# Seven blocks of queries in each pass of the unit loop, in place of one

## The chip, the cores and the metric

The kernel runs on one core of a Trainium2 chip. The metric is the time of one execution in device microseconds (us), the median of several runs. Engines are named as the profile names them: PE (matmul), PEld (its weight loads), DVE (vector), ACT (scalar, activations), POOL (GpSimd), SP (the queue that issues DMAs). A "q" behind an engine's name (ACTq, SPq) marks an instruction of its sequencer: a register operation, a branch, a semaphore operation or the issue of a DMA.

## The reference

x has 2 batches of 4096 tokens with 256 features. The first half is an attention with 16 heads of 16 features, whose weights are not a softmax but a sigmoid:

```
x_norm = layernorm(x, gamma, beta)
q, k = l2_normalize(x_norm @ w_q), l2_normalize(x_norm @ w_k);  v = x @ w_v      (per head)
resonance = 0.5 + 0.5 * tanh((q k^T - 0.27) * 15)
modulation = resonance * gate_q * gate_k        (gates: 0.25 + 0.75 sigmoid(q . g_q), the same for k)
x = layernorm(x + (modulation @ v) @ w_o + b_o)
```

The second half is a feed-forward network on each token, y = down(silu(gate(x)) * up(x)) with 704 hidden features, whose inputs and weights are rounded to 4-bit blocks of 16, and another layernorm of x + y.

## The kernel before, in words

Every engine has its own program; semaphores tie them together. There are three stages. The first projects 16 blocks of 512 tokens and stores q, k, v and the gates in DRAM. The second, the attention, takes nearly all of the time. The third finishes the last four tiles of tokens.

The attention is cut into 64 **units**: 16 blocks of 512 queries (index j, 8 per batch), and in each of them 4 groups of heads (index g). In a unit PE computes the scores of 4 heads against 32 tiles of 128 keys (`scores`, line 1257), ACT turns them into sigmoids (line 696), and PE sums them with v (`sums`, line 1267). This goes in 44 steps: a step's ACT instruction waits for the scores (`b_sc`), and PE's scores two steps later wait for that ACT instruction (`b_act`). At the end of a unit DVE takes the sums out of PSUM (`end_unit`, line 972, the instruction that writes `fs`); there are 64 of these, so their starts mark off the units. SP then stores `fs` (line 497), loads the gates (line 521), and loads the next unit's keys, queries and values (`load_unit`, lines 472 to 478).

Beside the attention, each unit from the fifth on carries one tile of 128 tokens of the feed-forward network for an earlier block. SP loads the tile's attention result into `m_f` (`load_sums`, line 503, after the stores of line 497 and the loads of line 521 in SP's program); PE needs it after step 7 of the unit (`begin_piece`, line 1279). PE's program is in a fixed order: while it waits for `m_f`, the scores of the next steps stand behind it.

The order over units is written by `units` (line 369), which every engine calls with its own `unit(j, g)`. The first two blocks (j = 0 and 1) are written out, with Python numbers for j. The other 14 go through a hardware loop of each engine (`fori`), whose register is j; its body holds one block, that is four units. Values that depend on j (the counts that semaphores are waited for, the addresses of DMAs) are computed in registers by the engine's sequencer. DVE also counts its own chain of dependent instructions: `before` (line 1020) sets the base of the count at the head of a pass, 4 units times 45 links further in each pass.

Of the kernel before, what the change touches and what calls it, by code (L numbers as in the profile page):

```python
# [23 lines left out]
HG = 4  # L24
NG = H // HG
NS = TB * 2 * H
NUNIT = B * NG * QB
# [58 lines left out]
LAST = {9: 0, 11: 1, 13: "gates", 15: 2, 17: 3}  # L86
NTAIL = HG
LOOP_FROM = 2

PT_BANKS = (7, 0, 1, 2)
# [5 lines left out]
L_CHAIN = 45  # L97
# [28 lines left out]
def build(nc, x, w_q, w_k, w_v, g_q, g_k, w_o, b_o, gamma, beta, w_gate, w_up, w_down, out):  # L126
# [12 lines left out]
    with ExitStack() as ctx:  # L139
# [229 lines left out]
        def units(fori, unit, before=lambda r: None):  # L369

            for j in range(LOOP_FROM):
                for g in range(HG):
                    unit(j, g)
            with fori(LOOP_FROM, NUNIT // HG) as j:
                before(j - LOOP_FROM)
                for g in range(HG):
                    unit(j, g)

        def begins(j, g):  # L380

            return not isinstance(j, int) or j >= 1

        def ends(j, g):

            return not isinstance(j, int) or HG * j + g > HG
# [367 lines left out]
        def _(dve):  # L754
            chain = Chain(dve, dve_step)
# [11 lines left out]
            def quantize(dst, src, w):  # L767

                nb = w // 16
                s3, xn3, t3 = (a.rearrange("p (n e) -> p n e", e=16) for a in (src, q_xn[:, 0:w], q_t[:, 0:w]))  # L770
                scale, inv = q_s[:, 0, 0, 0:nb], q_s[:, 0, 1, 0:nb]
                xn, e, t = q_xn[:, 0:w], q_e[:, 0:w], q_t[:, 0:w]
                after(dve.tensor_reduce(scale, s3, AX_X, ALU.max, apply_absolute_value=True))
                after(dve.tensor_scalar(scale, scale, 1 / 6, QUANT_EPS, ALU.mult, ALU.max))
                after(dve.reciprocal(inv, scale))
                after(dve.tensor_scalar(inv, inv, TIE_DOWN, None, ALU.mult))
                after(dve.tensor_tensor(xn3, s3, bcast(inv, 16), ALU.mult))

                after(dve.tensor_scalar(e.bitcast(I32), xn.bitcast(I32), EXPONENT, None, ALU.bitwise_and))
                after(dve.tensor_scalar(e, e, ROUNDER, ROUNDER, ALU.mult, ALU.max))  # L780
                after(dve.tensor_tensor(t, xn, e, ALU.add))
                after(dve.tensor_tensor(t, t, e, ALU.subtract))
                return dve.tensor_tensor(dst.rearrange("p (n e) -> p n e", e=16), t3, bcast(scale, 16), ALU.mult)
# [87 lines left out]
            at = chain.n  # L871
# [10 lines left out]
            def keep_last():  # L882

                for i, what in enumerate(LAST.values()):
                    dve.wait_ge(a_last, i + 1)
                    if what == "gates":
                        wait(dve, a_outg, 16 * (NBLK - 1))
                        ins = dve.tensor_copy(gT[:, :], ps[0:H, C_BANK, :])
                    else:
                        ins = dve.tensor_copy(last_pt[what], bank16(C_BANK))  # L890
                    ins.then_inc(a_lastev, 1)
# [27 lines left out]
            def end_transposes(k):  # L919
                for half in range(2):  # L920
                    dve.wait_ge(l_H, 2 * k + half + 1)
                    if half == 0:
                        dve.tensor_copy(m_hqT[:, 0:4, :].rearrange("p j n -> p (j n)"), ps[:, C_BANK, :])\
                           .then_inc(l_hT, 1)
                    else:
                        dve.tensor_copy(m_hqT[:, 4, :], ps[:, C_BANK, 0:P])  # L926
                        dve.tensor_copy(m_hqT[0:FR, 5, :], ps[0:FR, C_BANK, P:2 * P]).then_inc(l_hT, 1)  # L927

            def end_tile(k, par):
                dve.wait_ge(l_D, k + 1)  # L930

                wait(dve, l_st[par], 16 * (k // 2))
                after_fin(dve.tensor_tensor(m_xo[:, par], ps[:, C_BANK, 0:D], m_x1[:, par], ALU.add), k)  # L933
                normalize(m_xo[:, par], m_xo[:, par]).then_inc(l_out, 1)
# [5 lines left out]
            def begin_tile(k, par):  # L940
                x1 = m_x1[:, par]
                dve.wait_ge(l_P, k + 1)
                dve.wait_ge(l_xb, k + 1)
                dve.tensor_tensor(x1, ps[:, C_BANK, 0:D], m_x[:, :], ALU.add).then_inc(l_r, 1)  # L944
                dve.wait_ge(l_r, k + 1)
                after(normalize(x1, x1))
                wait(dve, l_X, k)
                to_grid(m_xq[:, :], x1, D, m_xs, m_xn[:, :], m_e[:, :], m_t[:, :]).then_inc(l_xq, 1)

            def gates(k):  # L950
                dve.wait_ge(l_X, k + 1)
                dve.tensor_copy(m_xqT[:, :, :].rearrange("p c n -> p (c n)"), ps[:, C_BANK, 0:D]).then_inc(l_xT, 1)
                for p in range(4):
                    cols = slice(p % 2 * FH, (p % 2 + 1) * FH)
                    if p < 2:
                        dve.wait_ge(l_sg, 2 * k + p + 1)
                        dve.tensor_tensor(m_tg[:, cols], ps[:, C_BANK, 0:FH], m_sg[:, cols], ALU.mult)\  # L957
                           .then_inc(l_ge, 1)
                    else:
                        dve.wait_ge(l_G, 4 * k + p + 1)  # L960
                        dve.wait_ge(l_ge, 4 * k + p)
                        dve.tensor_tensor(m_hb[:, cols], ps[:, C_BANK, 0:FH], m_tg[:, cols], ALU.mult)\  # L962
                           .then_inc(l_ge, 1)
                dve.wait_ge(l_ge, 4 * k + 4)
                wait(dve, l_H, 2 * k)
                to_grid(m_hq[:, :], m_hb[:, :], F, q_s[:, 0], q_xn[:, :], q_e[:, :], q_t[:, :]).then_inc(l_hq, 1)
# [7 lines left out]
            def keep_weights(i):  # L974

                dve.wait_ge(c_wt, i + 1)
                if i < 2:
                    ins = dve.tensor_copy(wdnT[:, 2 * i:2 * i + 2, :].rearrange("p j n -> p (j n)"), ps[:, C_BANK, :])
                elif i == 2:
                    dve.tensor_copy(wdnT[:, 4, :], ps[:, C_BANK, 0:D])  # L980
                    ins = dve.tensor_copy(wdnT[0:FR, 5, :], ps[0:FR, C_BANK, D:2 * D])
                else:
                    c, part3 = divmod(i - 3, 3)
                    if part3 < 2:
                        ins = dve.tensor_copy(wguT[:, c, part3 * F:part3 * F + 512], ps[:, C_BANK, :])
                    else:
                        for m in range(2):
                            dve.tensor_copy(wguT[:, c, m * F + 512:m * F + 640], ps[:, C_BANK, m * P:(m + 1) * P])
                        for m in range(2):
                            ins = dve.tensor_copy(wguT[:, c, m * F + 640:(m + 1) * F],  # L990
                                                  ps[:, C_BANK, 2 * P + m * FR:2 * P + (m + 1) * FR])
                ins.then_inc(c_wev, 1)

            def unit(j, g):
                u = HG * j + g
                if ends(j, g):
                    end_transposes(u - HG - 1)
                if begins(j, g):
                    begin_tile(u - HG, g % 2)
                if ends(j, g):  # L1000
                    end_tile(u - HG - 1, (g - 1) % 2)
                if begins(j, g):
                    gates(u - HG)
                if isinstance(j, int) and j == 0:
                    if g == 0:
                        keep_last()
                        dve.wait_ge(s_ffn, 16 * FFN_LOADS)
                    if g < 2:
                        for n in (range(0, W_FIRST), range(W_FIRST, DC + NW))[g]:
                            rows, w = (wdn[:, n, :], F) if n < DC else (wgu[:, n - DC, :], D)  # L1010
                            quantize(rows, rows, w).then_inc(w_q_done, 1)
                            dve.wait_ge(w_q_done, n + 1)
                    if g == 2:
                        for i in range(9):
                            keep_weights(i)
                end_unit(u)

            at = [0]

            def before(r):  # L1020
                at[0] = chain.n
                chain.start(at[0] + r * HG * L_CHAIN)

            units(dve.Fori, unit, before)
            assert chain.n == HG * L_CHAIN, chain.n
            chain.start(0)
            chain.n = at[0] + (NUNIT // HG - LOOP_FROM) * HG * L_CHAIN
            k = NT - NTAIL - 1
# [433 lines left out]
```

## Time and profile before

| | us |
|---|---|
| median of 3 runs | 4456.29 |
| lowest, highest run | 4455.4, 4465.12 |
| the profiled execution's own time | 4458.66 |
| its span, first to last instruction | 4456.9 |

| engine | busy us | share of the span |
|---|---|---|
| PE | 4149.7 | 93% |
| ACT | 4023.4 | 90% |
| DVE | 1561.7 | 35% |
| POOL | 159.3 | 4% |

The profile is of one execution. Register operations, branches, semaphore operations and the issue of DMAs are not counted as busy. The first stage ends some 320 us into the span, the attention some 4374 us into it. In the list of idle times, `A <- B` says that A was idle until B was done; "issue" stands for idle time in which the engine waited for nothing that the profile shows. PEclk is the granted share of TensorE's full clock.

### The profile page before, as it was taken

To read this page: it belongs to the slowest core of one execution; us is meant where nothing else is said; L and a number is where in the kernel's file an instruction comes from. 1 tells how busy PE (TensorE), PEld (TensorE's weight loads), DVE (VectorE), ACT (ScalarE), POOL (GpSimd) and SP (SyncE) were. 2 spreads that over 40 slices of the span, in tenths; PEclk is the share of its full clock that TensorE was granted. 3 is DMA by queue.
4 is the path that set the end of the run, shared out by engine and by line. 5 is a ranking of instruction groups with operands and counts; after the bars stand their busy time and mean duration, and the time that the engine had idled before them with its cause. 6 is when DMAs were issued, how large, how long until landed. Compare 5 with 4: busy or idle time off the path is not lost.

```text
span 4456.9 us, 80908 instructions
## 1 busy us (share of the span) xinstructions
PE 4149.7 (93%) x28776; PEld 1293.5 (29%) x28776; DVE 1561.7 (35%) x4540; ACT 4023.4 (90%) x3271; POOL 159.3 (4%) x120
## 2 busy tenths in 40 slices
PE   7978899999999999999999999999999999999997
PEld 5641222222222222222222222222222222222223
DVE  6754023332333233233332333233323323333236
ACT  4669999999999999999999999999999999999993
POOL 2330000000000000000000000000000000000001
PEclk9999999999999999999999999999999999999998
DMA  3454444334433443344334433443344334433440
GB/s 111 126 124 75 69 75 69 61 62 77 77 57 59 77 77 57 59 77 77 56 61 75 77 56 60 76 77 58 58 76 77 56 61 77 77 54 62 76 81 13
DMA packets 180058, 315.51 MB, mean 71 GB/s; under 512 B 65264, under 2 KB 141808, under 8 KB 154608
## 3 DMA queue, kind: packets, MB, share of 16 engines
q1 hardware_dynamic: 179568, 309.41, 41.2%
q8 instruction: 255, 4.18, 0.4%
q14 instruction: 235, 1.93, 0.2%
HBM read 266.82 MB, written 42.47 MB: 69 GB/s over the span
## 4 chain that ended last, share of the span: by engine, by line
PE 68%; ACT 17%; issue 9%; DVE 4%; SPq 1%; DMA 1%; POOL 0%; ACTq 0%; POOLq 0%; DVEq 0%
PE ps L1267 35%; PE ps L1257 19%; ACT room L696 16%; PE ps L1294 7%; PE ps L1317 4%; DVE room L848 1%; DMA m_f<-fused_t 1%; PE ps L1212 0%; DVE st L802 0%; DVE xnT L838 0%; PE ps L1223 0%; PE ps L1307 0%; SPq L521 0%; PE ps L1204 0%; DVE sm L763 0%
## 5 line engine op out<-in xcount | busy, mean ns | idle before, releaser
L696 ACT ACTIVATE room<-ps 128x1024 f32<-128x1024 f32 (+1 forms) x2816 | 3792.5, 1415 | 235.9 <-PE ps L1257 184.3
L1267 PE MATMUL ps<-room,vt 128*32 128x512 f32 x16384 | 2070.4, 606 | 0.0
L1257 PE MATMUL ps<-qs,room 64*128 64x512 f16 x8198 | 1335.6, 385 | 243.6 <-ACT room L696 221.4
L1257 PEld LDWEIGHTS ps<-qs,room 64*128 64x128 f16 x8198 | 311.1, 94 | 1800.6 <-ACT room L696 1141.6
L1267 PEld LDWEIGHTS ps<-room,vt 128*32 128x32 f32 x16384 | 390.4, 109 | 959.8 <-issue 959.8
L1294 PE MATMUL ps<-wguT,m_xqT 128*128 128x352 f32 x960 | 348.2, 485 | 0.0
L957 DVE TENSOR_TENSOR vz<-ps,vz 128x352 f32<-128x352 f32 x120 | 63.0, 525 | 757.7 <-ACT vz L706 757.7
L962 DVE TENSOR_TENSOR vz<-ps,vz 128x352 f32<-128x352 f32 x120 | 63.0, 525 | 595.8 <-PE ps L1294 595.8
L1317 PE MATMUL ps<-wdnT,wqk 128*128 128x256 f32 x720 | 198.9, 404 | 0.6 <-DVE wqk L927 0.6
L1294 PEld LDWEIGHTS ps<-wguT,m_xqT 128*128 128x128 f32 x960 | 162.6, 189 | 105.2 <-issue 54.3
L590 POOL TENSOR_TENSOR m_x<-m_x,bo 128x256 f32<-128x256 f32 x60 | 43.7, 728 | 3946.9 <-DMA m_x<-in_L_attn_x_dram 3946.9
L1317 PEld LDWEIGHTS ps<-wdnT,wqk 128*128 128x128 f32 x720 | 121.8, 188 | 56.8 <-issue 46.6
L944 DVE TENSOR_TENSOR m_x<-ps,m_x 128x256 f32<-128x256 f32 x60 | 25.5, 425 | 313.2 <-PE ps L1279 313.2
L972 DVE TENSOR_TENSOR fs<-ps,gqb 128x512 f32<-128x512 f32 x64 | 44.3, 692 | 254.4 <-PE ps L1267 254.4
L1204 PE MATMUL ps<-wqk,xnT 128*128 128x512 f32 x256 | 125.3, 612 | 6.8 <-DVE xnT L838 6.8
L933 DVE TENSOR_TENSOR wv<-ps,m_x 128x256 f32<-128x256 f32 x60 | 25.5, 425 | 292.5 <-PE ps L1317 292.5
L926 DVE COPY wqk<-ps 128x128 f32<-128x128 f32 x60 | 17.5, 292 | 254.4 <-PE ps L1308 254.4
L658 ACT COPY room<-ps 128x512 f32<-128x512 f32 x64 | 37.4, 585 | 75.0 <-PE ps L1212 40.6
L1279 PE MATMUL ps<-wo,m_f 128*128 128x256 f32 x240 | 67.8, 405 | 4.6 <-DMA m_f<-fused_t 4.6
L1212 PE MATMUL ps<-wv,xT 128*128 128x256 f32 x256 | 72.0, 404 | 0.0
L582 POOL TENSOR_TENSOR room<-room 128x2048 f16<-128x2048 f32 x16 | 65.3, 4084 | 1.8 <-ACT room L637 1.5
L764 DVE TENSOR_TENSOR m_ln<-m_ln 128x1 f32<-128x1 f32 x360 | 57.4, 159 | 19.8 <-DVE m_ln L763 8.2
(172 smaller groups left out, 2209.1 us busy)
## 6 DMA issues: line engine op xcount, KB each, us to landing
room<-k_parts SPq DMA_DIRECT2D x520, 256.0 KB, 9.3
vt<-v_gated SPq DMA_DIRECT2D x65, 1024.0 KB, 17.5
qs<-q_parts SPq DMA_DIRECT2D x520, 32.0 KB, 10.3
gqb<-q_gates SPq DMA_DIRECT2D x256, 64.0 KB, 2.1
room<-in_L_attn_x_dram SPq DMA_DIRECT2D x16, 512.0 KB, 4.3
v_gated<-vz SPq DMA_DIRECT2D x64, 128.0 KB, 2.1
fused_t<-fs SPq DMA_DIRECT2D x256, 32.0 KB, 1.6
q_parts<-room SPq DMA_DIRECT2D x30, 256.0 KB, 2.8
```

Source lines behind the costliest of these rows:

```text
L582: pool.tensor_tensor(part[1], qk[par][:, :, :], part[0], ALU.subtract).then_inc(a_lo, 1)
L696: act.activation(res[:, c, o:o + m, :], ps[:, o:o + m, :], ACT.Sigmoid, scale=2 * SHARP / QK_UP ** 2, bias=-2 * SHARP * THRESH).then_inc(b ...
L764: after(dve.tensor_tensor(t, t, ha, ALU.mult))
L957: dve.tensor_tensor(m_tg[:, cols], ps[:, C_BANK, 0:FH], m_sg[:, cols], ALU.mult)\
L962: dve.tensor_tensor(m_hb[:, cols], ps[:, C_BANK, 0:FH], m_tg[:, cols], ALU.mult)\
L1204: pe.matmul(ps[:, 4 + t % 2, :], xnT[:, c, tok], wqk[:, c, :], start=c == 0, stop=c == DC - 1)
L1212: ins = pe.matmul(ps[:, 6, 0:D], xT[:, c, tok], wv[:, c, :], start=c == 0, stop=c == DC - 1)
L1257: ins = pe.matmul(ps[:, BANK[n % 2] + i, :], ks[o:o + HROWS, par, h // 2, kt * P:(kt + 1) * P], qs[o:o + HROWS, par, h // 2, :], start=Tru ...
L1267: ins = pe.matmul(ps[32 * h:32 * h + 32, SUM_BANK, :], vt[:, par, n * HD:n * HD + 32], r, start=kt == 0, stop=kt == KT - 1, skip_group_che ...
L1279: ins = pe.matmul(c_ps[:, 0:D], m_f[:, c, :], wo[:, c, :], start=c == 0, stop=c == DC - 1)
L1294: ins = pe.matmul(c_ps[:, 0:FH], m_xqT[:, c, :], wguT[:, c, p * FH:(p + 1) * FH], start=c == 0, stop=c == DC - 1)
L1317: ins = pe.matmul(c_ps[:, 0:D], m_hqT[0:w, j, :], wdnT[0:w, j, :], start=j == 0, stop=j == FT_FULL)
```

## The change

The loop's body holds seven blocks (28 units) in place of one (4 units), and the loop makes two passes in place of 14. The register is now the number of the pass, r, and j is 7 r + 2 + i for the i-th block of the body. DVE's count advances by 7 times as much from pass to pass. Every engine's loop changes, since all call `units`. The work of a unit and its order stay.

```diff
@@ constants
 LOOP_FROM = 2
+BODY = 7
@@ units
-            with fori(LOOP_FROM, NUNIT // HG) as j:
-                before(j - LOOP_FROM)
-                for g in range(HG):
-                    unit(j, g)
+            with fori(0, (NUNIT // HG - LOOP_FROM) // BODY) as r:
+                before(r)
+                for i in range(BODY):
+                    for g in range(HG):
+                        unit(r * BODY + (LOOP_FROM + i), g)
@@ block.vector
             def before(r):
                 at[0] = chain.n
-                chain.start(at[0] + r * HG * L_CHAIN)
+                chain.start(at[0] + r * BODY * HG * L_CHAIN)

             units(dve.Fori, unit, before)
-            assert chain.n == HG * L_CHAIN, chain.n
+            assert chain.n == BODY * HG * L_CHAIN, chain.n
```

## Rows read from the trace of the kernel before

**Rows 1.** The page, part 4: shares of the chain that ended last, by engine.
```profile
PE 68%; ACT 17%; issue 9%; DVE 4%; SPq 1%; DMA 1%; POOL 0%; ACTq 0%; POOLq 0%; DVEq 0%
```
**Rows 2.** Timeline of DVE: ends of units (start us, us, what, idle before).
```profile
626.65 0.69 DVE L972 TENSOR_TENSOR fs<-ps,gqb 128x512 f32<-128x512 f32 x1 [2.45 <-PE ps L1267]
...
813.63 0.69 DVE L972 TENSOR_TENSOR fs<-ps,gqb 128x512 f32<-128x512 f32 x1 [2.45 <-PE ps L1267]
...
1063.13 0.69 DVE L972 TENSOR_TENSOR fs<-ps,gqb 128x512 f32<-128x512 f32 x1 [2.43 <-PE ps L1267]
...
1130.82 0.69 DVE L972 TENSOR_TENSOR fs<-ps,gqb 128x512 f32<-128x512 f32 x1 [2.45 <-PE ps L1267]
...
1317.91 0.69 DVE L972 TENSOR_TENSOR fs<-ps,gqb 128x512 f32<-128x512 f32 x1 [2.43 <-PE ps L1267]
...
1384.57 0.69 DVE L972 TENSOR_TENSOR fs<-ps,gqb 128x512 f32<-128x512 f32 x1 [2.45 <-PE ps L1267]
...
2080.24 0.69 DVE L972 TENSOR_TENSOR fs<-ps,gqb 128x512 f32<-128x512 f32 x1 [2.43 <-PE ps L1267]
...
4119.87 0.69 DVE L972 TENSOR_TENSOR fs<-ps,gqb 128x512 f32<-128x512 f32 x1 [2.43 <-PE ps L1267]
```
**Rows 3.** Line 375, the loop: branches (ns min/median/max, first and last start us).
```profile
L375 POOLq COMPARE_BRANCH  x14: 40/45/50, 1009.2 to 4320.2; - x14
...
L375 SPq COMPARE_BRANCH  x14: 48/53/53, 1029.1 to 4339.9; - x14
...
L375 ACTq COMPARE_BRANCH  x14: 40/45/50, 1060.3 to 4371.1; - x14
...
L375 PEldq COMPARE_BRANCH  x14: 83/3593/3843, 1061.2 to 4372.0; - x14
...
L375 DVEq COMPARE_BRANCH  x14: 55/63/63, 1063.2 to 4374.0; - x14
```
**Rows 4.** The chain of waits around one end of a pass (start us, us, what).
```profile
2077.44 0.04 ACTq L375
2077.48 3.06 issue
2080.54 0.06 ACTq L375
...
2080.65 0.06 ACT room L696
```
**Rows 5.** Line 696, ACT's sigmoids: one cause of their idle time (us, times).
```profile
  issue: 34.7, 13
```
**Rows 6.** The page, part 3: queues that load instructions (blocks, MB, share of the engines).
```profile
q8 instruction: 255, 4.18, 0.4%
q14 instruction: 235, 1.93, 0.2%
```
**Rows 7.** Stretches: us, busy us of PE, PEld, DVE, ACT, POOL, PEclk, DMA share, GB/s.
```profile
1062.80:1077.80 15.00, 11.36 (x72) 2.62 (x68) 1.86 (x4) 11.27 (x9) 0.73 (x1) 0.77 0.54 98
1317.60:1332.60 15.00, 11.28 (x76) 3.05 (x73) 1.86 (x4) 12.22 (x9) 0.73 (x1) 0.89 0.56 99
326.00:1063.00 737.00, 676.97 (x4954) 180.75 (x4950) 220.48 (x623) 704.38 (x540) 9.91 (x9) 1.00 0.43 69
```
**Rows 8.** Line 1279: one cause of PE's idle time before it (us, times).
```profile
  DMA m_f<-fused_t: 5.1, 8
```
**Rows 9.** Tile m_f: time to landing, all units; its matmul's first weight load in two units.
```profile
DMA to landing us min/median/max: 2.1/2.4/4.5
...
L1279 PEld LDWEIGHTS ps<-wo,m_f x4: 186/190/190, 823.5 to 824.1; 128*128 128x128 f32 x4
...
L1279 PEld LDWEIGHTS ps<-wo,m_f x4: 186/190/190, 2095.4 to 2096.0; 128*128 128x128 f32 x4
```
**Rows 10.** Timeline of SP: the issue of the load into m_f in the same two units.
```profile
819.94 0.40 SPq L503 DMA_DIRECT2D m_f<-fused_t  x1
...
2087.97 0.39 SPq L503 DMA_DIRECT2D m_f<-fused_t  x1
```
**Rows 11.** Line 497, SP's stores of fs: their register operations (ns min/median/max).
```profile
L497 SPq FUSED_REGOPS  x238: 37/37/228, 814.4 to 4313.9; - x119
```

## The prediction

> **What bounds the kernel now.** I read the chain of waits first. PE and ACT hold most of it, and 9% goes to "issue", waits for nothing that the profile shows [rows 1]: the two engines drive each other step by step, and something that is no work stands between. Next I read the ends of the units as a clock. Three units that are written out take 813.63 - 626.65 = 186.98 us, 62.33 each. The next four, from 813.63 to 1063.13, take 249.50, or 62.38 each. They are the first pass of the loop, which is entered without a jump back [rows 2]. The unit after that ends at 1130.82, 67.69 us later, though it does the same work. From the end of the first pass to the end of the thirteenth (1063.13 to 4119.87) there are 12 passes, 3056.74 us or 254.73 each. So a pass that begins with a jump back costs 254.73 - 249.50 = **5.23 us** more than the one that is fallen into. That difference is all that the change can work on.
>
> The loop's own line tells where it arises. On ACT the branch takes 0.045 us [rows 3], yet ACT's next instruction starts 3.06 us after it [rows 4], and PE has nothing to do until ACT's first sigmoid of the pass is done. ACT's idle time with cause "issue" is 34.7 us in 13 pieces, 2.7 us each [rows 5], and 13 is the number of jumps taken (14 branches, the last one not). PE's own branch takes 3.59 us in the median and 0.083 us at the shortest [rows 3]; I read the short one as the last, which isn't taken. Instructions arrive in blocks through queues of their own (255 and 235 in the run) [rows 6], and I take the gap for the time to fetch the block at the head of the body. The pause has a tail: in the 15 us behind it the granted clock is 0.77 or 0.89, that is half speed (1.2 GHz of 2.4) for about 7 or 3.4 us, where the 737 us before the first jump have 1.00 throughout [rows 7]. The two kinds of jump differ as the clock does: 67.69 us for the unit with 0.77, 1384.57 - 1317.91 = 66.66 for the one with 0.89 [rows 2].
>
> **The change, part by part.** It *removes* 12 of the 13 jumps back on every engine: one is left, between two passes of 28 units. It removes 12 times the loop's register operations and branches too, which are inside the 5.23. POOL's branch (0.045 us) and SP's (0.053 us) come some 50 and 30 us ahead of the end of their pass [rows 3], in time in which both wait, and are worth nothing. DVE's comes after its last instruction of the unit and lies beside ACT's gap. Gross gain: 12 x 5.23 = 62.8 us.
>
> What it *moves* is cover. In the first unit of a looped pass the load into `m_f` is issued at 2087.97, 7.73 us after the end of the unit before (2080.24) [rows 2, 10]; with the median 2.4 us to landing [rows 9] it is there 10.1 us after that end. PE comes to it only 15.2 us after (2095.4) [rows 9], because it was held up. Where nothing holds PE up it comes at +9.9 us (823.5 against 813.63) [rows 2, 9]. There the load was issued at 819.94, +6.3 us [rows 10], and was in time by 1.2 us with the median landing. So in the 12 units that lose the pause, the landing of `m_f` is late next. Bounds: nothing, if SP issues as in the unit at 813; 7.73 + 4.5 (the slowest landing) - 9.9 = 2.3 us, or 28 us in all, if it stays as late as now and lands at its slowest each time. I stand near the lower end, since the row at 813 is just such a unit, a block's first without a jump: PE lost 5.1 us in 8 such waits [rows 8] over the 47 units that have no pause before them, 0.11 each, and 12 x 0.11 = 1.3 us. The waits that are there already lie partly in the mean of 254.73 and hardly in the 249.50, and they don't go away: 5.1 x 48/60 = 4.1 us of the gross gain stays.
>
> What it *adds* are longer expressions: 7 r + 2 + i where a register held j. On ACT and PE each wait's count is one register operation ahead of a wait; that work is done while the engine runs or waits for the other, and if it took two operations in place of one it would still be covered by an ACT instruction of about a microsecond. On SP the register work stands before each DMA, and ten of them (four stores, four gates, `m_x`, `m_f`) come before `m_f` lands. The commonest operation takes 0.037 us, the longest, at the head of a block, 0.228 [rows 11]. Bounds: nothing, if each expression is folded into one operation as now; 12 x (0.228 - 0.037) = 2.3 us later if all twelve operations up to `m_f` became the longest. I take nothing: r enters each value as j did, as a multiple plus a constant, save in the division of j by 8, which is already in the longest one. The longer body itself costs nothing that I can see: PE's blocks stream in through the 249.50 us without a jump, and four units pass there without a gap.
>
> Sum: 62.8 - 4.1 - 1.3 = **57.4 us** less. Against the profiled execution's 4458.66 (span 4456.9) that is 4401.3; the median of the runs is 4456.29, 2.4 lower, and against it the time is **4398.9 us**.
>
> **Rivals.** *The pause stays*: what stops ACT is the change of block, which comes 14 times still, and only the branch itself goes. For it: the pause is seen only where both happen. Against it: at 813.63 the block changes without a jump, and the unit takes no longer. The gain is then 12 x 0.045 = 0.5 us, time 4455.8. The Trainium skill, in "Advanced Engine Details and Errata", section Control Flow Timing, gives about 108 ns for a compare-and-branch; by that price alone the gain would be an estimated 12 x 0.108 = 1.3 us and the time 4455.0. The trace has less than that for the branch of ACT and thirty times as much for what follows it.
>
> *The clock falls anyway*: full speed over 1700 us isn't granted, and the half-speed stretches come about as often as now. The one with 0.77 costs by the pair above about 2 x 1.03 = 2.1 us; 12 of them are 25 us back: 4424. Against it: 737 us at 1.00 with PE 92% busy, and each fall follows a pause [rows 7].
>
> *SP's addresses become the wait* (the side that is slower): every looped unit, 56 of them, has `m_f` landing at about +9.4 (the issue halfway between the two units read, +7.0, and the median 2.4) against a need at +9.9, so a slack of 0.5. With the upper bound of 2.3 us more, each unit loses 1.8, 101 us in all against 62.8 gained: 4494. It decides from 0.5 + 62.8 / 56 = 1.6 us more per unit. For it: the slack is small, and PE's queue behind the wait holds the scores. Against it: the operation at the block's head already has j to divide, and it comes once, the others being 0.037 in the median.
>
> **How the numbers follow.** The forecast has 0.91; the pause that stays 0.03; the clock 0.02; SP's addresses 0.04. For the range: if all waits for `m_f` went, the gain would be 62.8 and the time 4393.5, and the median of the runs can be 1 to 3 us off (4455.4 to 4465.12 in three); the low end is 4389. Upwards, late landings of half the upper bound (14 us) give 4412, which is the high end. Less than 2 in 10 lies outside. A measurement tells 0.2% (9 us) from no change: faster by more is the forecast and the clock's case, 0.93; within it the pause that stays, 0.03; slower 0.04.
>
> **What would show it.** After: in ACT's idle time the cause "issue" with one piece of about 2.7 us in place of 13; two branches per engine on the loop's line; ends of units 62.3 to 62.4 us apart through 28 units and one step of about 67; PEclk 1.00 through each pass, one fall between them; `m_f` issued at about +6.3 to +7 in each unit and PE's waits for it 5 to 12 us in all. I am wrong if steps of 67 us still come every fourth unit (the pause stays), if PEclk falls without a pause before it, or if the time to `m_f`'s issue grows by a microsecond or more and PE waits for it in most units.

## The result, and the profile after

The changed kernel takes 4403.85 us in the median of 4 runs (4401.77 to 4404.74), the kernel before 4458.88 over its runs beside them (4455.4 to 4465.12): a ratio of 0.9873, with a 95% interval of 0.9858 to 0.9888, or 55.0 us less. The profiled execution took 4404.2 us, its span 4402.4.

The rows that answer to those of before. In the page's part 4, the chain has 8% "issue" where [rows 1] has 9%; in part 3, queue 14 loads 153 blocks of instructions where [rows 6] has 235.

```profile
q8 instruction: 232, 3.80, 0.4%
q14 instruction: 153, 1.25, 0.1%
...
PE 68%; ACT 16%; issue 8%; DVE 4%; DMA 2%; SPq 2%; POOL 0%; ACTq 0%; POOLq 0%; DVEq 0%
```

The ends of units in DVE's timeline (start us, us, what), to be read beside [rows 2]:

```profile
814.83 0.69 DVE L974 TENSOR_TENSOR fs<-ps,gqb 128x512 f32<-128x512 f32 x1 [2.45 <-PE ps L1269]
...
1064.53 0.69 DVE L974 TENSOR_TENSOR fs<-ps,gqb 128x512 f32<-128x512 f32 x1 [2.43 <-PE ps L1269]
...
1376.41 0.69 DVE L974 TENSOR_TENSOR fs<-ps,gqb 128x512 f32<-128x512 f32 x1 [2.45 <-PE ps L1269]
...
1440.07 0.69 DVE L974 TENSOR_TENSOR fs<-ps,gqb 128x512 f32<-128x512 f32 x1 [2.44 <-PE ps L1269]
...
2315.14 0.69 DVE L974 TENSOR_TENSOR fs<-ps,gqb 128x512 f32<-128x512 f32 x1 [2.44 <-PE ps L1269]
...
2564.63 0.69 DVE L974 TENSOR_TENSOR fs<-ps,gqb 128x512 f32<-128x512 f32 x1 [2.43 <-PE ps L1269]
...
2630.52 0.69 DVE L974 TENSOR_TENSOR fs<-ps,gqb 128x512 f32<-128x512 f32 x1 [2.44 <-PE ps L1269]
```

From 2315.14 to 2564.63 four units take 249.49 us, the clean pass of before. The one unit behind a jump takes 65.89 us (2564.63 to 2630.52). A third kind is new: the unit from 1376.41 takes 63.67 us and has no jump before it.

The jump itself: the loop's line (number, then ns min/median/max, first and last start) and the chain around the one jump, beside [rows 3] and [rows 4].

```profile
L376 ACTq COMPARE_BRANCH  x2: 40/45/50, 2561.5 to 4316.1; - x2
...
L376 PEldq COMPARE_BRANCH  x2: 83/1897/3711, 2562.7 to 4317.3; - x2
```

```profile
2561.55 0.05 ACTq L376
2561.60 2.46 issue
2564.06 0.08 ACTq L376
```

One branch of PE is long (3711 ns) and the last one short. ACT stands still for 2.46 us, less than the 3.06 of [rows 4]. Among the causes of ACT's idle time "issue" no longer appears; the one piece is booked to PE there.

The clock (stretches, with PEclk behind the five busy times), beside [rows 7]:

```profile
337.00:2564.00 2227.00, 2103.58 (x15080) 587.88 (x15072) 712.91 (x2087) 2129.13 (x1638) 23.38 (x32) 1.00 0.43 69
2564.40:2579.40 15.00, 11.82 (x80) 3.40 (x78) 1.99 (x5) 12.97 (x10) 0.73 (x1) 0.89 0.59 104
2573.00:4319.00 1746.00, 1668.44 (x11846) 475.63 (x11842) 573.13 (x1706) 1664.68 (x1283) 21.83 (x30) 1.00 0.42 69
```

Full speed is granted through 2227 and 1746 us, and falls only behind the jump. Last, the load into `m_f`: the view of this tile (what PE waited for before line 1281, in us and times, and issue to landing), and SP's issues in two units, beside [rows 8 to 10].

```profile
  DMA m_f<-fused_t: 11.3, 16
...
DMA to landing us min/median/max: 2.1/2.7/5.7
```

```profile
1070.36 0.40 SPq L505 DMA_DIRECT2D m_f<-fused_t  x1
...
1383.80 0.40 SPq L505 DMA_DIRECT2D m_f<-fused_t  x1
```

The waits for `m_f` have grown from 5.1 us in 8 to 11.3 us in 16. The issue comes 5.83 us after the end of the unit before in the first of these units (1064.53) and 7.39 in the second (1376.41), which is the one of 63.67 us.

Where the 55 us come from can be counted over the ends of units. From the end of the first block to the end of the last unit the profiled executions take 3808.7 us before and 3752.9 after, 55.8 less. Behind a jump there were 13 steps that were together 64.3 us over the usual 62.38; now there is one, 3.5 us over. Other long steps (over 62.45 us) were 5, together 3.4 us over; now they are 14, together 7.9 us over. That is 60.8 us gained, 4.5 given back, and 0.5 left over, the scatter of the ordinary steps.

### The profile page after: what moved, and what is told of

It is laid out like the page before. It is cut to its first block, busy times and chain, and to the rows that moved or that the text cites. A ratio compares the mean times of both kernels' runs of the same rounds, so it can differ in the third digit from the quotient of the medians.

```text
span 4402.4 us, 80654 instructions
## 1 busy us (share of the span) xinstructions
PE 4119.8 (94%) x28776; PEld 1290.5 (29%) x28776; DVE 1562.0 (35%) x4540; ACT 4021.6 (91%) x3271; POOL 159.4 (4%) x120
## 4 chain that ended last, share of the span: by engine, by line
PE 68%; ACT 16%; issue 8%; DVE 4%; DMA 2%; SPq 2%; POOL 0%; ACTq 0%; POOLq 0%; DVEq 0%
PE ps L1269 34%; PE ps L1259 19%; ACT room L698 15%; PE ps L1296 8%; PE ps L1319 4%; DMA m_f<-fused_t 2%; DVE room L850 1%; SPq L523 1%; SPq L499 1%; PE ps L1214 0%; PE ps L1281 0%; DVE st L804 0%; DVE xnT L840 0%; PE ps L1225 0%; PE ps L1206 0%
## 5 line engine op out<-in xcount | busy, mean ns | idle before, releaser
L766 DVE TENSOR_TENSOR m_ln<-m_ln 128x1 f32<-128x1 f32 x360 | 57.4, 160 | 14.3 <-DVE m_ln L765 2.1
```

What stands on the lines that cost most here:

```text
L766: after(dve.tensor_tensor(t, t, ha, ALU.mult))
```

## The experiments

Each set was run beside the kernel before on one chip; its median there was 4452.39 us in the first set, 4453.73 in the second and 4455.24 in the third. Ratios are to those.

**Fewer and no jumps.** `BODY` is the one constant that is edited.

```diff
-BODY = 7
+BODY = 2
```

> Body of two blocks, seven passes, six jumps back. Theory (a price per jump, 55.0 us for 12 jumps = 4.6 us each): 7 jumps fewer than before, 32 us less, about 4427 us. Rival (what counts is a long body, or the seven in particular, not the number of jumps): a time near one of the two kernels, 4459 or 4404.

4412.28 us, ratio 0.9913 (0.9896 to 0.9929): 40.1 us less for 7 jumps fewer, where 32 were expected. The changed kernel's ratio would be 4396 us on this chip, so the time is near neither of the two kernels: the number of jumps decides, not a long body. But the price of one isn't fixed. Of its 6 jumps two cost only 1.8 us. In DVE's timeline and in the stretches behind the jumps, one of each kind:

```profile
1312.00 0.69 DVE L974 TENSOR_TENSOR fs<-ps,gqb 128x512 f32<-128x512 f32 x1 [2.43 <-PE ps L1269]
...
1376.13 0.69 DVE L974 TENSOR_TENSOR fs<-ps,gqb 128x512 f32<-128x512 f32 x1 [2.45 <-PE ps L1269]
...
1812.83 0.69 DVE L974 TENSOR_TENSOR fs<-ps,gqb 128x512 f32<-128x512 f32 x1 [2.43 <-PE ps L1269]
...
1879.80 0.69 DVE L974 TENSOR_TENSOR fs<-ps,gqb 128x512 f32<-128x512 f32 x1 [2.45 <-PE ps L1269]
```

```profile
1313.00:1323.00 10.00, 8.35 (x68) 2.35 (x68) 1.17 (x3) 9.52 (x9) 0.73 (x1) 1.00 0.50 111
1812.00:1827.00 15.00, 12.18 (x76) 2.65 (x68) 1.87 (x4) 11.51 (x9) 0.72 (x1) 0.77 0.53 95
```

The first step is 64.13 us and the clock stays at 1.00; the second is 66.97 and the clock falls. So the pause alone costs 1.8 us here, and the half-speed stretch up to 2.8 us more where it follows (ACT's pauses in the two differ by 0.15 us). The other jumps fit: behind one more, of 64.14 us, the clock has 1.00; behind those of 65.6 and 65.8 us it has 0.89 over 15 us, and behind the last, of 66.90 us, 0.77.

```diff
-BODY = 7
+BODY = 14
```

> Body of fourteen blocks, one pass, no jump. Theory: the last jump goes too, which shows as one unit of 65.9 us in place of 62.4, so 3 to 5 us less than with seven blocks, about 4400 us. Rival (a longer body costs more in loading instructions or in late transfers): 4404 or more.

4388.19 us, ratio 0.9858 (0.9841 to 0.9874), 64.2 us less than before. Beside the second set the changed kernel gains 52.1, so this is some 12 us more, where 3 to 5 were expected; the two intervals overlap. The profiled executions differ by 12.9 us from the end of the first block to the end of the last unit: 3.5 are the last jump, 7.0 the other long steps, and the remaining 2.4 are spread over the ordinary steps. With a single pass j is a number in every unit, and SP's register operations vanish. In the unit that follows the end at 1124.64 the load into `m_f` is issued 5.66 us after it, 4.94 in the median of all units, against 6.29 in the changed kernel, and the long steps are 4 with 0.9 us in place of 14 with 7.9. PE still waits 7.1 us for `m_f`, in 15, but only four steps come out over 62.45 us. Four units then take 249.31 us:

```profile
1124.64 0.69 DVE L974 TENSOR_TENSOR fs<-ps,gqb 128x512 f32<-128x512 f32 x1 [2.46 <-PE ps L1269]
...
1373.95 0.69 DVE L974 TENSOR_TENSOR fs<-ps,gqb 128x512 f32<-128x512 f32 x1 [2.46 <-PE ps L1269]
```

```profile
1130.30 0.39 SPq L505 DMA_DIRECT2D m_f<-fused_t  x1
```

**One engine alone.** `units` gets the number of blocks as an argument, and each engine's call passes its own.

```diff
-        def units(fori, unit, before=lambda r: None):
+        def units(fori, unit, before=lambda r: None, body=BODY):
...
-            units(act.Fori, unit)
+            units(act.Fori, unit, body=7)
-            units(pe.Fori, unit)
+            units(pe.Fori, unit, body=1)
```

> Only ACT's loop has the body of seven blocks; PE, DVE, POOL and SP have one block and jump 13 times. Theory (ACT and PE both stand still at the jump, side by side, and PE alone would hold the step up nearly as long): PE comes back some 0.4 us earlier than ACT let it, so about 5 us less than before, 4454 us, and half-speed stretches at each jump as before. Rival (ACT's pause is the whole cost): about 4404 us.

4432.87 us, ratio 0.9955 (0.9938 to 0.9972), 19.5 us less. Neither the 5 nor the 50: ACT's jump is about a third of the price. Without its own jump ACT works off the two steps whose scores PE had issued ahead while PE stands still. My 0.4 us took the moment at which PE comes back, and forgot that lead. The half-speed stretch, expected at each jump, is absent at four of the 13. The clock tells the kinds of step apart here too:

```profile
1063.28 0.69 DVE L974 TENSOR_TENSOR fs<-ps,gqb 128x512 f32<-128x512 f32 x1 [2.43 <-PE ps L1269]
...
1129.99 0.69 DVE L974 TENSOR_TENSOR fs<-ps,gqb 128x512 f32<-128x512 f32 x1 [2.44 <-PE ps L1269]
...
1317.07 0.69 DVE L974 TENSOR_TENSOR fs<-ps,gqb 128x512 f32<-128x512 f32 x1 [2.42 <-PE ps L1269]
...
1381.21 0.69 DVE L974 TENSOR_TENSOR fs<-ps,gqb 128x512 f32<-128x512 f32 x1 [2.44 <-PE ps L1269]
```

```profile
1063.00:1078.00 15.00, 12.42 (x76) 3.10 (x73) 1.86 (x4) 10.40 (x8) 0.73 (x1) 0.77 0.59 102
1317.00:1332.00 15.00, 12.18 (x95) 3.65 (x94) 3.58 (x12) 12.82 (x10) 0.73 (x1) 1.00 0.57 98
```

66.71 us where the clock falls, 64.14 where it doesn't.

> Only PE's loop has the body of seven blocks; the other engines jump 13 times. Theory (side by side): ACT's pause stays and PE waits for it, 0 to 7 us less than before, 4452 to 4459 us. Rival (PE's pause is the whole cost): about 4404 us.

4456.76 us, ratio 1.0009 (1.0000 to 1.0019): nothing gained. ACT's pause holds PE whether PE jumps or not; ACT's idle time keeps its 13 pieces of "issue":

```profile
  issue: 32.5, 13
```

So the pauses do lie side by side: with ACT's alone all of the price is left, and with PE's alone about two thirds of it.

> PE's and ACT's loops with seven blocks, those of DVE, POOL and SP with one block and 13 jumps. Theory (DVE's pause of 2.9 us lies in time in which PE has other steps to do, POOL and SP have none): as the changed kernel within 4 us, about 56 us less than before. Rival (DVE's pause holds PE's next steps up): a remainder of 1 us or more in each of 13 jumps, 13 us or more above the changed kernel.

4406.79 us, ratio 0.9895 (0.9878 to 0.9911); the changed kernel beside it took 4401.59. DVE still jumps 13 times:

```profile
L376 DVEq COMPARE_BRANCH  x14: 55/63/63, 1061.0 to 4319.6; - x14
```

and the unit behind such a jump, from 1310.64 to 1373.04, takes 62.40 us, like any other. DVE's, POOL's and SP's pauses cost nothing by themselves. The 5.2 us above the changed kernel are a little over the 4 expected, and the two intervals overlap; in the profiled execution, which took 4402.79, each long step but the one behind PE's and ACT's jump is one in which `m_f` landed late, so DVE's pause doesn't show as a pause anywhere. Five of these eleven steps, 6.2 us over the usual one in sum, are the first of a pass; whether the jump has a part in the late landing isn't shown.

**The jump without the fetch.** One block in the body and 14 passes, as before the change; each of four engines marks at the head of a pass where its jump back goes.

```diff
-BODY = 7
+BODY = 1
...
+        def hinted(eng):
+            return lambda a, b: nc.Fori(a, b, engines=OrderedEngineSet([eng.engine]), hint_back_edge=True)
...
-            units(act.Fori, unit)
+            units(hinted(act), unit)
```

4392.41 us, ratio 0.9862 (0.9846 to 0.9879), 61.3 us less than before and 9.2 less than the changed kernel beside it (4390.77 to 4397.0 us against 4397.98 to 4403.4), with all 13 jumps in place. The loop's line, with the mark as an instruction of its own at the head of each pass, the chain around one jump and the clock over the attention:

```profile
L380 ACTq BRANCH_PREFETCH_HINT  x14: 31/31/50, 809.6 to 4054.8; - x14
...
L380 ACTq COMPARE_BRANCH  x14: 44/49/73, 1059.5 to 4304.1; - x14
...
L380 PEldq COMPARE_BRANCH  x14: 88/360/381, 1060.7 to 4305.2; - x14
```

```profile
2058.09 0.05 ACTq L380
2058.14 0.16 issue
2058.29 0.03 ACTq L380
```

```profile
337.00:4304.00 3967.00, 3772.11 (x26908) 1062.87 (x26900) 1286.25 (x3795) 3797.71 (x2923) 45.06 (x62) 1.00 0.43 69
```

ACT's next instruction comes 0.16 us after the branch instead of 3.06 [rows 4], PE's branch takes 0.36 us in place of 3.59 [rows 3], and the clock stays at 1.00 throughout. The branch, the register operations and the change of block are still there; what is gone is the fetch at the jump. In each of the 13 jumps of the kernel before, two of the smaller blocks of instructions start 0.7 to 1.0 and 1.1 to 1.3 us behind the start of ACT's branch, inside its pause, and one of the larger blocks 1.8 to 2.2 us behind it. ACT goes on 1.51 to 1.55 us behind the end of the second smaller block each time, while its pause varies from 3.1 to 3.4 us. What fills the 1.5 us isn't shown. In the marked kernel no block moves between ACT's branch and its next instruction; here is the count of all DMA packets from 2058 to 2059 us:

```profile
DMA packets 0, 0.00 MB, mean 0 GB/s; under 512 B 0, under 2 KB 0, under 8 KB 0
```

That settles the cause: the pause is the fetch, and not the jump. POOL bears it out. Its pass has ten instructions and its loop has no mark, and already in the kernel before its next instruction comes 0.12 us behind each of its 13 jumps. When and by what way the marked kernel has the head of the body at hand isn't shown.

The Trainium skill, in "Runtime: NRT & Kernel Launch", section Instruction fetch mechanics, says that a taken branch whose target isn't among the blocks at hand forces a fetch before execution can go on. The trace agrees, and adds a price: 2.4 to 3.4 us on ACT, from the start of the branch to the next instruction, over the profiled executions of this study.

**The load that comes late.** SP's four gate loads go behind the load into `m_f`.

```diff
-                for h in range(HG):
-                    sp.dma_start(gqb[32 * h:32 * h + 32, :], ...).then_inc(b_gq, 16)
                 if begins(j, g):
...
                     load_sums(m_f[:, :, :], j - 1, g).then_inc(l_f, 16)
+                for h in range(HG):
+                    sp.dma_start(gqb[32 * h:32 * h + 32, :], ...).then_inc(b_gq, 16)
```

The changed kernel itself, once more beside it:

> The changed kernel once more, beside the others of this set. On the chip of the first set the kernel before took 4452.4 us; 0.9873 of that is 4396 us. The same ratio within 0.2% is expected by every theory.

4401.59 us, ratio 0.9877 (0.9860 to 0.9893), as expected.

> The changed kernel with SP's four gate loads put behind the load into m_f, which is then issued some 2 us earlier. Theory (with the pauses gone, the late landing of m_f is what still lengthens units: 14 longer steps, 7.9 us in sum, in the changed kernel's profile): PE's 16 waits for m_f go nearly all, 5 to 8 us less than the changed kernel. Rival (m_f then waits for the landing of the stores of fs in its place, or the gates come late): no gain, within 2 us.

4392.81 us, ratio 0.9861 (0.9844 to 0.9877), 8.8 us less than the changed kernel beside it (4389.66 to 4397.76 us against 4397.98 to 4403.4). `m_f` is issued 4.35 us after the end of a unit in the median and lands sooner too, and PE never waits for it: apart from the one behind the jump, no step from the second block on is over 62.45 us.

```profile
DMA to landing us min/median/max: 2.1/2.2/3.1
```

> The kernel before with the gate loads behind the load into m_f, 13 jumps and their pauses kept. Theory (in the kernel before PE came to m_f late by the pause in 13 units, so a late landing there cost nothing, and only the other units' 5 longer steps, 3.4 us in sum, can go): 3 to 4 us less than before. Rival (m_f cost as much before as after the change, and the 9 us it gave there are to be had here too): 8 us or more less.

4450.87 us, ratio 0.9990 (0.9981 to 0.9999), 4.4 us less: the same edit is worth half as much where the pauses are. With `m_f` out of the way this run prices the jumps cleanly: 13 steps of 66.5 to 67.7 us, together 62.4 us over the usual step, 4.80 each.

**Both causes together.**

> One block in the body, the mark for the jump, and the gate loads behind the load into m_f. Theory (two separate causes, the fetch at the jump and the late m_f): the 5 longer steps of the marked kernel, 1.8 us in sum, and its wait of 3.4 us in all go, so 2 to 4 us less than with the mark alone, about 63 us less than before. Rival (the mark's own fetches disturb the transfers): no less than with the mark alone.

4390.35 us, ratio 0.9852 (0.9837 to 0.9867), 64.9 us less than before. The marked kernel's long steps are gone; the 3.6 us that it gains beyond the mark alone, on another chip, are inside the intervals.

> Fourteen blocks in the body, one pass, and the gate loads behind the load into m_f. Theory: no jump, no late m_f, and every unit at the 62.32 us of the units written out, where the loops have 62.37; that is 64 units times 0.05, or 3 us, less than the marked kernel with the gates behind, and about 66 us less than before. Rival (nothing is left to gain): the time of that kernel within 1 us.

4388.94 us, ratio 0.9848 (0.9835 to 0.9862), 66.3 us less than before and the lowest ratio here. The marked kernel with a body of one block isn't told apart from it by these intervals. Both ratios lie 0.002 to 0.003 below the changed kernel's 0.9873 and 0.9877; the intervals still overlap, and the chips differ.

## Why the prediction was right

Forecast were 57.4 us less; the runs gave 55.0, in an interval from 50 to 63, and 4403.85 us lies 5 us above the 4398.9: 2.4 of them are the gain, and 2.6 come from the kernel before, which took 2.6 us more beside the changed kernel than in the runs that the forecast had.

**The price of a jump** was taken as 5.23 us on the mean of a pass, 62.8 in all; less the 4.1 us of waits that this mean holds, 58.7 or 4.9 a jump. It holds: 60.8 us are gone from the steps behind jumps, which were 4.95 us over the usual one in the kernel before, and the kernel with early `m_f` puts a jump at 4.80. The reason, a fetch at the head of the body, was inferred from a gap; the mark shows it. That the two pauses are one price and not two is shown by the loops changed alone. The prediction has DVE's pause "beside ACT's gap"; by [rows 3] DVE's first branch starts at 1063.2 us, 2.9 us behind ACT's, so its pause lies mostly behind ACT's. It costs nothing all the same, as the kernel with longer bodies for PE and ACT shows. The tail of half speed is a part of the price, and a large one: over the two kernels that had both kinds a jump costs 1.7 to 1.8 us without it and 3.2 to 4.9 with it.

**The cover that goes** was the step that was under-sized. "12 x 0.11 = 1.3 us" for the twelve units that lose the pause was close: their long steps come to 1.8 us. The "4.1 us of the gross gain" stands for waits that were there already, and these were 3.4 us of long steps. What the sum has no term for is that such waits grew: outside those twelve units the long steps come to 6.1 us after the change. So 4.5 us were given back where 1.3 were forecast, and 2.1 more than the 58.7 were gained behind the jumps. The two errors partly cancel, and that the gain came out within 2.4 us is in part luck. `m_f` took 2.7 us to land in the median where it had taken 2.4 [rows 9], and up to 5.7. Some of this varies from one execution to the next: the changed kernel's second profile has 10.4 us of PE's waits for it, in 11, against 11.3 in 16.

**The register work on SP** was taken as nothing, and that holds for the change from one body to another: `m_f` is issued 6.29 us after the end of a unit in the median, 6.85 before. It isn't nothing against a body with no register, where it is 4.94.

**The rivals.** The pause that stays with the change of block is refuted by the changed kernel's changes of block that have no jump (the unit from 1064.53 takes 62.39 us), and by the marked kernel, where every block changes with a jump and without a pause. The price that the Trainium skill gives for a compare-and-branch, in "Advanced Engine Details and Errata", section Control Flow Timing, was no measure of the gain: the branch was never the cost. The clock that falls anyway is refuted by the 2227 us at 1.00. SP's addresses become a wait of some units only, and the upper bound of 2.3 us never came; what late landings there are cost 7.9 us, not 101.

## What to carry to other kernels

A loop can pay for each jump back: on the engines that drive each other in step a fetch of instructions that no work hides, 2.4 to 3.4 us on ACT here, and behind it, in most cases here, a stretch in which PE has half speed. POOL, with ten instructions in a pass, doesn't pay it. Fewer jumps, a single pass, or the mark at the head of the pass cut or remove it; the mark does it without a longer program, and these runs don't tell it from writing everything out (61.3 and 64.2 us less). And when a regular pause goes, look for the transfer that it had been covering: moving one load ahead of four that nobody was waiting for gave another 9 us.

## What had not been expected

ACT's pause at a jump is of two lengths, from the start of the branch to the next instruction: 3.0 to 3.4 us where ACT's body has one block and no mark, 2.4 to 2.8 us where it is longer. The queue of the smaller blocks moved two of them during ACT's pause at each jump of the kernel before and one in the kernel with two blocks per pass (part 3 of the page for just these stretches: packets, MB, share):

```profile
q14 instruction: 2, 0.02, 1.8%
```

```profile
q14 instruction: 1, 0.01, 1.2%
```

Why it was two there was not tried. The shorter pause goes with the lower price of a jump in the kernel with two blocks.

The late landings of `m_f` keep to places in the program. Among the units of the changed kernel's loop the two slowest are 28 units apart, the length of the body (the units from 1440.07 and 3192.42, 4.8 and 5.7 us from issue to landing), and the same two are the slowest of the loop in its second profile. In each of them, in the first profile, a block of the larger kind started 1.4 or 1.6 us behind the issue. These are PE's blocks: 255 of them are loaded in the kernel before and in the one with only ACT's loop changed, 232 in the one with only PE's changed. In the kernel with a single pass the pattern is clearer. Seven of its 60 loads into `m_f` had such a block 1.0 to 1.8 us behind the issue and took 4.8 to 5.5 us; the others took 2.5 in the median and 4.75 at most. That loads of instructions delay `m_f` is a reading of this pattern; no run took it apart.

A late load can bring the clock down as a jump does. In the changed kernel's second profile PE waited 2.18 us for `m_f` at 3202 us, and the stretch around it has the clock at 0.89; that unit took 65.84 us.

```profile
3202.24 2.07 PE L1281 MATMUL ps<-wo,m_f 128*128 128x256 f32 x4 [2.18 <-DMA m_f<-fused_t]
```

```profile
3195.00:3210.00 15.00, 12.82 (x83) 4.11 (x82) 5.32 (x24) 10.82 (x9) 0.73 (x1) 0.89 0.90 136
```
